# Gate masks on GpSimd, the mixed pair turned in two phase halves, and the convolution's bias on ScalarE

## The reference, cut to what matters

```python
# x: (32, 32, 512), cond_128: (32, 128)
h = gelu(cond @ W0 + b0); h = gelu(h @ W1 + b1); att = softmax(h @ W2 + b2)   # (32, 8)
mixed = einsum('boi,bih->boh', einsum('bk,koi->boi', att, weight), x) + (att @ bias_k)[:, :, None]
q, k, v = (nan_to_num(mixed @ sign(w).T * scale) for w in (q_w, k_w, v_w))    # 32 heads of 16, 8 for k and v
a = softmax(q @ k.T / 4) @ v                       # per sample and head, 32 x 32 scores
x = x + nan_to_num(a @ sign(o_w).T * scale)
y = conv1d(x, w, taps=9, groups=4) + (cond @ c_weight.T)[:, :, None] + bias[None, :, None]
logits = y @ router_w.T + router_b                 # 8 experts per token
top2 -> gates = softmax over the two best; w = gates spread over the 8 experts
out = x + einsum((y @ A.T) * w, Bm) * 0.5          # rank 16 per expert
```

## Time and profile before

| | |
|---|---|
| three executions | 121.7, 122.1, 124.11 us; median 122.1 |
| profiled execution | 121.39 us |
| its span, first to last instruction | 119.6 us |
| TensorE (PE) busy | 105.5 us, 88% |
| VectorE (DVE) busy | 92.7 us, 77% |
| ScalarE (ACT) busy | 62.7 us, 52% |
| GpSimd (POOL) busy | 48.9 us, 41% |
| granted clock of TensorE | 0.999 of full speed |

### The profile page before, as it was taken

The page is one execution under the profiler, slowest core; times in us unless marked ns, Lnnn a source line. Parts: engine busy times, 40 slices in busy tenths (PEclk is TensorE's granted clock), DMA queues, the critical chain, the costliest instruction groups (busy, mean ns, idle before and its releaser), DMA issues. The chain is left out here.

```text
span 119.6 us, 3340 instructions
## 1 busy us (share of the span) xinstructions
PE 105.5 (88%) x1264; PEld 78.0 (65%) x1264; DVE 92.7 (77%) x244; ACT 62.7 (52%) x138; POOL 48.9 (41%) x74
## 2 busy tenths in 40 slices
PE   0979999979999899996869999899999899988870
PEld 0766698769999798974748577475756645644510
DVE  0158998839989999959989999979757685857851
ACT  4549889967484859395646163735244004031400
POOL 1020910025018639879999939693721000000000
PEclk9999999999999999999999999999999999999999
DMA  3899999950000000200393883997299859997032
GB/s 86 262 313 413 427 374 428 401 181 3 0 5 1 0 0 0 93 0 30 119 196 104 172 180 121 212 189 144 88 256 194 130 194 212 189 258 289 35 134 103
DMA packets 19237, 19.54 MB, mean 163 GB/s; under 512 B 1684, under 2 KB 14868, under 8 KB 18836
## 3 DMA queue, kind: packets, MB, share of 16 engines
q1 hardware_dynamic: 18068, 17.22, 55.7%
q10 hardware_dynamic: 1152, 2.10, 4.8%
HBM read 15.12 MB, written 4.20 MB: 162 GB/s over the span
## 5 line engine op out<-in xcount | busy, mean ns | idle before, releaser
L434 POOL TENSOR_TENSOR probs<-probs,row_inv 128x512 f32<-128x512 f32 x16 | 16.8, 1052 | 5.3 <-DVE row_inv L970 3.8
L1321 PE MATMUL halves<-mixed_hi,qkv_sign 128*128 128x256 f32 x72 | 17.3, 285 | 0.0
L1322 PE MATMUL halves<-mixed_lo,qkv_sign 128*128 128x256 f32 x72 | 16.7, 277 | 0.0
L1321 PEld LDWEIGHTS halves<-mixed_hi,qkv_sign 128*128 128x128 f32 x72 | 13.5, 188 | 0.4 <-issue 0.2
L1399 PE MATMUL halves<-wo_sign,attn_hi 128*128 128x512 f32 x32 | 13.6, 425 | 0.0
L1322 PEld LDWEIGHTS halves<-mixed_lo,qkv_sign 128*128 128x128 f32 x72 | 13.5, 188 | 0.0
L416 POOL TENSOR_TENSOR keys_diag<-kv,keymask 128x512 f32<-128x512 f32 x8 | 8.8, 1107 | 10.9 <-DVE calm L935 10.7
L1399 PE MATMUL halves<-wo_sign,attn_lo 128*128 128x512 f32 x32 | 12.6, 392 | 0.0
L966 DVE TENSOR_REDUCE row_sum<-probs 128x16 f32<-128x512 f32 x16 | 10.6, 671 | 1.5 <-ACT probs L590 1.4
L452 POOL TENSOR_TENSOR x_all<-x_all,o_out 128x512 f32<-128x512 f32 x7 | 9.0, 1280 | 6.3 <-DVE o_out L983 6.3
L590 ACT ACTIVATE probs<-probs 128x512 f32<-128x512 f32 x16 | 9.8, 628 | 3.3 <-DVE probs L960 3.3
(11 more groups left out here) (144 smaller groups left out, 223.4 us busy)
## 6 DMA issues: line engine op xcount, KB each, us to landing
rows_sb<-x_turned SPq DMA_DIRECT2D x18, 256.0 KB, 5.1
x_all<-in_x_rows SPq DMA_DIRECT2D x4, 512.0 KB, 9.1
x_turned<-x_all ACTq DMA_DIRECT2D x8, 256.0 KB, 2.5
out_rows<-x_all SPq DMA_DIRECT2D x8, 256.0 KB, 3.7
qkvT_sb<-in_qkvT SPq DMA_DIRECT2D x4, 384.0 KB, 5.9
rows_sb<-in_qkv_rows SPq DMA_DIRECT2D x1, 1536.0 KB, 9.8
qkv_sign<-x_turned SPq DMA_DIRECT2D x6, 256.0 KB, 5.2
rows_sb<-in_wo_rows SPq DMA_DIRECT2D x1, 1024.0 KB, 14.0
```

What stands on the lines that cost most here:

```text
L434: pool.tensor_tensor(probs[:, t % 2, h, :, :], probs[:, t % 2, h, :, :], row_inv[:, t % 2, h, :].unsqueeze(2).to_broadcast([P, HALF, TOKENS]),
L1321: mm(dst, w, mixed_hi[:, ph, cols(i % 2, PAIR)], start=(ph == 0 and n % 2 == 0), stop=False)
L1322: last = mm(dst, w, mixed_lo[:, ph, cols(i % 2, PAIR)], start=False, stop=(ph == PHASES - 1 and n % 2 == 1))
```

## The change

Four things are changed in the functions. `gate_masks(t)` moves from VectorE to GpSimd, as four small instructions in place of two, and takes over the weighted sum of the masks that `gate_weights` did. `turn_mixed(i)` still has two instructions, but each now turns two phases of both tiles, and `high_part(i, b)` waits for its own half alone. `bias_conv(t)` moves to ScalarE and runs one instruction per sample, four of 128x128 with the bias as a column. New waits guard the buffers that cross engines. Nearly every list of calls is then written in another order; the last lines of the diff show ScalarE's first two entries. The added functions are GpSimd's `gate_masks` and ScalarE's `bias_conv`, the removed ones VectorE's.

```diff
+            def gate_masks(t):
+                iota = misc_sb[:, MISC["iota"]]
+                pool.wait_ge(gate_idx_ready, t + 1)
+                pool.tensor_copy(gate_idx_f[:, t % 2, :], gate_idx[:, t % 2, 0:2]).then_inc(idx_f_ready, 1)
+                pool.wait_ge(idx_f_ready, t + 1)
+                pool.tensor_scalar(gate_mask[:, t % 2, 0, :], iota, gate_idx_f[:, t % 2, 0:1], None, ALU.is_equal).then_inc(gate_mask_ready, 1)
+                pool.wait_ge(gate_exp, t + 1)
+                pool.tensor_scalar(gate_mask[:, t % 2, 1, :], iota, gate_idx_f[:, t % 2, 1:2], gate_e[:, t % 2, :],
+                                   ALU.is_equal, ALU.mult).then_inc(gate_mask_ready, 1)
+                pool.wait_ge(gate_mask_ready, 2 * (t + 1))
+                reached(pool, gated_ready, t - 1)
+                pool.tensor_tensor(gate_w[:, t % 2, :], gate_mask[:, t % 2, 0, :], gate_mask[:, t % 2, 1, :],
+                                   ALU.add).then_inc(gate_w_ready, 1)
...
             def high_part(i, b):
-                act.wait_ge(mixed_turned, 2 * i + 2)
+                act.wait_ge(mixed_turned, 2 * i + b + 1)
...
+            def bias_conv(t):
+                act.wait_ge(conv_done, t + 1)
...
+                reached(act, convT_done, 2 * (t - 1))
+                for s in range(PER_TILE):
+                    last = nc.scalar.activation(conv_y[t % 2][:, s, :], ps_conv(t)[:, cols(s, STEPS)], ACT.Identity,
+                                                bias=conv_bias[:, PER_TILE * t + s:PER_TILE * t + s + 1])
+                last.then_inc(conv_biased, 1)
...
             def turn_mixed(i):
...
-                for a in range(2):
-                    v.transpose(mixed[:, i % 2, :, cols(a, P)].rearrange("p k (q o) -> p q k o", q=PER_TILE),
-                                mixing(i)[:, :, cols(a, P)].rearrange("p q (k r) -> p q k r", k=PHASES)).then_inc(mixed_turned, 1)
+                for b in range(2):
+                    v.transpose(mixed[:, i % 2, 2 * b:2 * b + 2, :].rearrange("p k (a q o) -> p q a k o", a=2, q=PER_TILE),
+                                mixing(i).rearrange("p q (a k r) -> p q a k r", a=2, k=PHASES)[:, :, :, 2 * b:2 * b + 2, :]
+                                ).then_inc(mixed_turned, 1)
...
-            def bias_conv(t):
...
-                v.tensor_tensor(conv_y[t % 2], ps_conv(t)[:, :].rearrange("p (s m) -> p s m", s=PER_TILE),
-                                conv_bias[:, cols(t, PER_TILE)].unsqueeze(2).to_broadcast([P, PER_TILE, STEPS]),
-                                ALU.add).then_inc(conv_biased, 1)
...
-            def gate_masks(t):
...
-                dve.wait_ge(gate_mask_ready, t + 1)
-                v.scalar_tensor_tensor(out=gate_w[:, t % 2, :], in0=gate_mask[:, t % 2, 1, :], scalar=gate_e[:, t % 2, :],
-                                       in1=gate_mask[:, t % 2, 0, :], op0=ALU.mult, op1=ALU.add).then_inc(gate_w_ready, 1)
...
+            sum_x(0)
             turn_shares()
```

More of the change, by code:

```diff
@@ L705, in _ @@
+            copy_probsT(2, 0)
             scale_qkv(3, 4)
             scale_qkv(3, 5)
[L707 removed]
+            attn_high(1)
+            exponents(4, 0)
+            copy_probsT(2, 1)
+            exponents(4, 1)
             store_x1(0)
[L709 to L712 removed]
             copy_probsT(3, 0)
+            copy_probsT(3, 1)
             attn_high(2)
[L715 removed]
             exponents(5, 0)
+            exponents(5, 1)
@@ L717, in _ @@
+            attn_high(3)
             store_x1(1)
             copy_probsT(4, 0)
-            exponents(5, 1)
-            attn_high(3)
+            exponents(6, 0)
             copy_probsT(4, 1)
-            exponents(6, 0)
+            store_x1(2)
+            bias_conv(0)
             exponents(6, 1)
-            store_x1(2)
             attn_high(4)
+            copy_probsT(5, 0)
+            copy_probsT(5, 1)
+            copy_convT(0)
             store_x1(3)
-            copy_convT(0)
-            copy_probsT(5, 0)
@@ L742, in _ @@
-            copy_probsT(7, 0)
+            bias_conv(2)
+            copy_probsT(7, 1)
+            store_x1(6)
             copy_convT(2)
-            copy_probsT(7, 1)
             copy_gatedT(1)
             attn_high(7)
+            bias_conv(3)
+            gate_exponent(2)
             copy_convT(3)
-            gate_exponent(2)
             copy_gatedT(2)
-            store_x1(6)
             store_x1(7)
             gate_exponent(3)
+            bias_conv(4)
+            bias_conv(5)
+            copy_convT(4)
@@ L1501, in _ @@
             project(1, 1)
+            conv_context()
             score(0)
@@ L1577, in _ @@
             turn_gated(4)
+            turn_gated(5)
             turn_conv(6)
@@ L1581, in _ @@
             convolve(7)
-            turn_gated(5)
+            ffn_down(5)
             turn_conv(7)
-            ffn_down(5)
             ffn_up(7)
```

301 lines of the change are left out of this document (140 added, 161 removed).

## The result

The changed kernel takes 123.03 us in the median of 17 executions, the kernel before 122.1 in 17 beside it. The ratio is 1.0092, with a 95% interval of 1.006 to 1.0123: 0.9% slower. I had forecast 121.4, 0.6% faster, with a range of 119.2 to 124.0. The profiled execution took 123.98 us, and TensorE's granted clock was halved at its very end; three more of the 17 have as low a mean clock (0.978 to 0.981) and took 123.9 us or more.

The account below looks back on a forecast made before the run. TensorE's list of matmuls was taken as the bound. 0 - 1.4 - 0.5 + 1.2 = -0.7 us took the profiled 121.39 to 120.7, carried over from the median of 122.1 to 121.4, range 119.2 to 124.0.

Parts of the forecast that it names:

- The start: 0: Program start: the halved turn and the earlier `sum_x(0)` gain nothing, since the first half was ready before its use.
- 56 to 79.4: -1.4: 56 to 79.4 us: TensorE's stops of 1.27 and 0.97 go, VectorE is next to be late, so 1.4 us faster.
- the third rival: VectorE's row operations were the bound, stops move to other turns, only +1.2 and -0.5 stay: 122.8 us, chance 0.12.
- 79.4 to 103.35: -0.5: 79.4 to 103.35 us: at most 0.85 us idle time to win, at most 0.6 lost to longer biases, so 0.5 faster.
- The bias on ScalarE: four in 1.14 us: Each tile's convolution bias: four overlapping activations of about 0.36 us take 1.14 us, where VectorE took 0.68: +0.46.
- The mask chain: 1.35 us: Index search to `gate_apply`: four GpSimd instructions and two handovers take 1.35 us instead of 0.84: +0.5.
- The tail: +1.2: Last tiles: longer bias +0.46, last mask chain +0.5, `turn_gated(5)` ahead of `turn_conv(6)` +0.25; from +0.4 to +1.9.
- The sum: Whole kernel: 0 - 1.4 - 0.5 + 1.2 = -0.7 us, carried over to a median of 121.4.
- The second rival: Tile 0's window is late behind `store_x1(0)`, holding up TensorE's and ScalarE's queues: 125.0 us, chance 0.12.

Follow-up runs that it names:

- e1: The kernel before with the mixed pair's turn by halves alone, no list changed: 122.37 us, ratio 1.003.
- e4: The changed kernel with its three edits (halved turn, masks on GpSimd, bias on ScalarE) taken out and its orders kept: 124.2 us, ratio 1.0172.
- e6: e4 with `store_x1(6)` moved later in ScalarE's list, behind `copy_convT(2)`, `copy_gatedT(1)` and `attn_high(7)`: 121.98 us, ratio 0.9892.
- e5: The changed kernel with `store_x1(6)` three places later in ScalarE's list: 122.78 us, ratio 0.998.
- e13: The changed kernel, edits whole, with only the tail of its lists in the order of the kernel before: 122.79 us, ratio 1.0037.
- e2: The kernel before with the gate masks alone moved to GpSimd, every other order as before: 124.02 us, ratio 1.0175.
- e12: The changed kernel measured again, nothing changed: 123.14 us, ratio 1.0089.
- e15: e6 measured again, nothing changed: 122.07 us, ratio 0.9983.
- e9: e6 with the tail of three engines' lists as in the kernel before: 121.06 us, ratio 0.9915.
- e16: e9 measured again, nothing changed: 121.16 us, ratio 0.9898.
- e11: The changed kernel with `store_x1(6)` behind `copy_convT(2)`, masks 4 to 7 and biases 6 and 7 on VectorE, and e9's tail: 121.25 us, ratio 0.9922.

## Why the prediction was wrong, step by step

**The start: 0.** `project(1, 0)` started at 25.52 before and at 25.78 and 25.72 in the changed kernel's two profiles. But over all profiles it lies between 25.41 and 25.85 with the whole turn and between 25.31 and 26.11 with the halved one, so nothing is shown. The time of e1 doesn't tell it from 0 either; its interval leaves room for a loss of up to 1 us. Right as far as is known.

**56 to 79.4: -1.4.** Nearly right in size, half wrong in mechanism. When `project_out(5)` ended at 81.83 in both, the changed kernel had `attend(6)` and `turn_probs(7, 0)` behind it as well, which is about 1.2 us. But only one of the two stops "had no cause left"; the other came back at the same moment on VectorE's row chain, as the third rival said of both. It stands there in all 14 profiles of the new order, with 1.23 to 1.32 us. `store_x1(0)` left at 57.21 (forecast: near 57), and `convolve(0)` started at 66.37 with no DMA wait, 1.1 us after the forecast 65.3.

**79.4 to 103.35: -0.5. This is the step that failed.** It came out at +1.0: of the 1.2 us only 0.17 were left at `convolve(6)`. I took the 0.85 us of idle time as what could be won, and bounded the loss by one longer bias for two tiles, 0.6. The trace has four stops instead, 2.10 us where 0.91 were. One, of 0.56, waits for a copy behind `store_x1(6)`. I had booked that store's earlier place as a gain: it left 6.45 us earlier, and 1.04 of them arrived at the reads. It was the same head-of-line block that I had found behind the earlier trace rows, moved to another tile; e4 shows it at 1.72 us. Two wait for ScalarE's longer bias, 0.68 and 0.40, but only the first is longer for it: with the bias on VectorE, e6 has 0.23 there, and at the second place more than the changed kernel, 0.66:

```profile
98.58 0.46 PE L1435 MATMUL halves<-misc_sb,woT_sb 64*128 64x64 f32 x8 [0.66 <-DVE woT_sb L1000]
```

The fourth, 0.46 ahead of `ffn_up(1)`, is in e6 as well. So of the 1.2 us of added idle time some 0.4 to 0.5 belong to the new order with the store moved (1.35 us of stops in e6), 0.56 to the store's place and 0.2 to the bias on ScalarE. I had put the order's own new waits at nothing. And I left out the window of tile 6. I had worked out tile 0's, not whether a later one was as close; in e5's profile it takes back a gain of 0.6 us.

**The bias on ScalarE: four in 1.14 us.** Measured 1.14, each 372 ns, where I had 0.36 us. `turn_conv(7)` came 0.44 later, as forecast, and `ffn_up(7)` only 0.27. The prediction had it that `ffn_up(7)` waited for the copy before; it didn't. The copy ended at 111.38, and `ffn_up(7)` followed `ffn_down(5)` without a stop at 111.60. The new order fills the wait with that `ffn_down(5)` and so hides 0.18; in the old order (e13) the longer bias shows in full, 3.69 against 3.24. By the Trainium skill, page "ScalarE: Activation LUTs", section "What ACT_TABLE_LOAD costs", four would take an estimated 1.27 us, worked out from its price of an activation with a pointer bias and its overlap; the trace lies 10% below that.

**The mask chain: 1.35 us.** Measured 1.36 here, and 1.36 in e2. The four instructions take 0.18, 0.31, 0.40 and 0.20 us, and follow each other after 0.29, 0.29 and 0.48, where I had 0.34 each; that the sum fits to 0.01 is luck. The last piece grew by 0.81, since the unexplained pause of 0.29 came with it.

**The tail: +1.2.** It was 1.65 us up to the start of the last `ffn_down` (1.42 in e12): +0.47 up to `convolve(7)` (forecast +0.25; 0.23 in e12), +0.27, +0.10 for `ffn_up(7)` itself, which took 1.19 us after its stop, and +0.81. The mechanism was right but for `ffn_up(7)`, and its size low. The profiled execution has 0.86 more in its last `ffn_down`, at the lower clock, and e12's has not.

**The sum.** With -0.17 and +1.65 it is +1.5 at the last `ffn_down` (+1.35 in e12) against -0.7. The medians lie only 0.9 us apart: the profile of the kernel before is 0.6 us faster than its median in the table, so the traces show the loss too large. Of the miss in the traces, 1.5 us are the stretch from 79.4 on, 0.2 to 0.45 the tail, and 0.2 the stretch before. The second rival (a late window, with queues held up behind a store) named the right mechanism at tile 0, where it didn't happen; the third (stops move to other turns) was nearest to the time, 122.8.

**What the change is made of,** by the table: its order from 57 us to `convolve(6)`, with `store_x1(6)` moved, is worth -0.7 to -0.9 us (e6, e15, e9, e16). With the store where the changed kernel has it and with the edits, -0.2 to +0.1 is left of that (seven profiles); with the store moved and the edits, -0.6 (e11). So the store's place costs most of it and the edits 0.1 to 0.4; e5's one profile, with its late window, stands outside this (+0.5). The tail's order costs +0.2 to +0.5, less the 0.18 it hides, the last bias +0.3, the last masks +0.5, and the pause ahead of the index search +0.3. The halved turn is worth nothing that these runs show. The two versions that beat both kernels, e9 and e11, keep the order of the middle and leave the last tiles' bias and masks on VectorE.
